# Attention scores of two heads at once on the two halves of TensorE's rows

## The reference

```
q, k, v = split(x @ qkv_w.T + qkv_b)          # per head 512 x 16
scores = q @ k.T * 16**-0.5, causal
attn = softmax(scores)
seq_out = attn @ v
x = layernorm(x + (seq_out + gated * mem_val) @ out_w.T + out_b)
x = layernorm(x + experts(x))
```

## Time and profile before

| | us |
|---|---|
| median of 3 runs | 828.99 (825.13 to 829.65) |
| profiled execution | 834.11 |
| its span | 832.4 |
| TensorE busy | 734.4 (88%) |
| VectorE busy | 603.8 (73%) |
| ScalarE busy | 351.0 (42%) |
| GpSimd busy | 422.3 (51%) |
| mean granted TensorE clock | 0.946 |

### The profile page before, as it was taken

The page is one execution under the profiler, slowest core; times in us unless marked ns, Lnnn a source line. Parts: engine busy times, 40 slices in busy tenths (PEclk is TensorE's granted clock), DMA queues, the critical chain, the costliest instruction groups (busy, mean ns, idle before and its releaser), DMA issues.

```text
span 832.4 us, 12395 instructions
## 1 busy us (share of the span) xinstructions
PE 734.4 (88%) x4004; PEld 495.0 (59%) x4004; DVE 603.8 (73%) x2105; ACT 351.0 (42%) x701; POOL 422.3 (51%) x334
## 2 busy tenths in 40 slices
PE   6993998898898998999898998878899899998995
PEld 3452655565565666565565664446677676776774
DVE  2344776778878888889688877736777877787785
ACT  2211555446454545555455555842242242232410
POOL 9200894996665676668476893424134042240410
PEclk9995999999998999999899997899999999999998
DMA  7899589675564574655734747220220302303000
GB/s 274 257 234 165 127 142 144 163 115 104 130 102 84 133 119 100 152 85 138 139 69 105 139 87 170 73 101 2 77 85 18 101 10 93 102 1 102 26 24 27
DMA packets 60420, 89.88 MB, mean 108 GB/s; under 512 B 8234, under 2 KB 37316, under 8 KB 60356
## 3 DMA queue, kind: packets, MB, share of 16 engines
q1 hardware_dynamic: 60356, 89.09, 47.7%
HBM read 54.72 MB, written 33.82 MB: 106 GB/s over the span
## 4 chain that ended last, share of the span: by engine, by line
PE 47%; DVE 23%; DMA 10%; POOL 9%; ACT 4%; issue 4%; SPq 2%; ACTq 0%; POOLq 0%; DVEq 0%
PE ps L1256 15%; PE ps L374 8%; PE ps L338 7%; PE ps L327 6%; PE ps L315 6%; DVE ps L468 5%; DMA Wm<-mem_scratch 3%; DVE Ob L516 3%; DMA Q<-MT 3%; DVE A L1390 3%; ACT X L1242 2%; PE ps L1221 2%; PE ps L232 1%; POOL Pr L612 1%; DVE Z L1276 1%
## 5 line engine op out<-in xcount | busy, mean ns | idle before, releaser
L468 DVE CUSTOM_DVE_ANT_0 ps<-ps,mask 128x256 f32<-128x256 f32 (+3 forms) x512 | 236.9, 509 | 31.8 <-PE ps L315 31.0
L411 ACT ACTIVATE Pr<-ps 128x512 f32<-128x512 f32 (+2 forms) x384 | 190.1, 528 | 114.8 <-PE ps L327 110.6
L327 PE MATMUL ps<-Q,K 98*128 98x256 f32 (+2 forms) x512 | 173.2, 380 | 28.9 <-DMA Q<-MT 21.9
L315 PE MATMUL ps<-K,Q 96*128 96x256 f32 (+2 forms) x512 | 157.9, 355 | 23.2 <-DVE nmax L468 22.5
L1256 PE MATMUL ps<-ew_hi,XT 128*128 128x512 f32 x512 | 176.2, 403 | 0.0
L1390 DVE SCALAR_TENSOR_TENSOR A<-ps,cw,A 128x256 f32<-128x256 f32 x256 | 123.6, 483 | 48.5 <-PE ps L1256 36.0
L327 PEld LDWEIGHTS ps<-Q,K 98*128 98x128 f32 x512 | 94.1, 197 | 104.8 <-ACT Pr L411 61.0
L612 POOL TENSOR_SCALAR_AFFINE_SELECT Pr<-Pr 128x512 f32<-128x512 f32 x128 | 88.3, 704 | 103.2 <-ACT Pr L411 100.8
L315 PEld LDWEIGHTS ps<-K,Q 96*128 96x128 f32 x512 | 103.0, 203 | 45.8 <-DVE nmax L468 28.3
L1256 PEld LDWEIGHTS ps<-ew_hi,XT 128*128 128x128 f32 x512 | 97.0, 189 | 21.2 <-issue 0.3
L1256 PE MATMUL ps<-ew_rest,XT 128*128 128x512 f32 x256 | 101.2, 395 | 0.0
(11 more groups left out here) (190 smaller groups left out, 1049.2 us busy)
## 6 DMA issues: line engine op xcount, KB each, us to landing
qk_scratch<-HL SPq DMA_DIRECT2D x32, 512.0 KB, 3.2
Q<-qk_scratch SPq DMA_DIRECT2D x96, 128.0 KB, 4.4
K<-qk_scratch SPq DMA_DIRECT2D x96, 128.0 KB, 5.7
Pr<-xT SPq DMA_DIRECT2D x8, 512.0 KB, 7.0
xraw<-xT SPq DMA_DIRECT2D x8, 512.0 KB, 6.4
mem_scratch<-Rl SPq DMA_DIRECT2D x16, 256.0 KB, 7.5
mv_scratch<-MV SPq DMA_DIRECT2D x32, 128.0 KB, 1.8
Wm<-mem_scratch SPq DMA_DIRECT2D x16, 256.0 KB, 9.3
```

Source lines behind the costliest of these rows:

```text
L315: last = nc.tensor.matmul(o, Q[0:STACK, hh, P * i:P * i + P], K[0:STACK, hh, 0:n], start=True, stop=True)
L327: last = nc.tensor.matmul(o, K[0:STACK + 2, hh, P * kt:P * kt + P], Q[0:STACK + 2, hh, T - n:T], start=True, stop=True)
L411: nc.scalar.activation(probs(g % 2, kt, heads[0], len(heads)), src, ACT.Exp, scale=SCALE).then_inc(s_exp, 1)
L468: last = nc.vector.tensor_tensor_reduce(out=scores, in0=scores, in1=mask[:, T - w:T], scale=1.0, scalar=NEG, op0=ALU.add, op1=ALU.max, acc ...
```

## The change

Scores use 64-row halves of the array. `STACK` is 48: head pairs stand one in rows 0 to 49 and one in rows 64 to 113 of `Q` and `K`, which have half as many column blocks. TensorE goes through the units in pairs (u, u + 1), and the two units' matmuls alternate between the halves and write to different banks. Max scores have four banks instead of three, so the outputs are turned in the values' bank and the maxima in the projections' bank. A pair of exp scores waits for all exponentials before it.

A projection is two pieces of three matmuls, at units 0 and 2, and 6 and 8, instead of one of six at units 4 and 10. Turning the maxima (unit 4) and turning the outputs (unit 8 instead of 10) stay on TensorE's list; the first now waits for VectorE's part of the projection before it. `HL`, `xhi` and `xlo` are held twice; the x split of a batch is done half a batch earlier. On VectorE the projection's part comes at units 4 and 10 instead of 5 and 11, the turned maxima at 5 instead of 4, and the normalising at 9 instead of 10. SyncE stores the two halves of `HL` apart, builds `Q` and `K` with eight DMAs a group instead of six (the same bytes), and writes the rows of maxima with four instead of two. The opening's memsets of `Q` and `K` shrink to two small ones of `K`.

```diff
-STACK = 96
+STACK = 48
+HALF = 64
-        S_ps, ST_ps = ps[0:2] + ps[7:8], ps[2:4]
-        O_ps, OT_ps, J_ps = ps[4:7]
-        M_ps = OT_ps
+        S_ps, ST_ps = [ps[0], ps[1], ps[7], ps[5]], ps[2:4]
+        O_ps, J_ps = ps[4], ps[6]
+        OT_ps, M_ps = O_ps, J_ps
...
-            return (2, [2 * (u - 8), 2 * (u - 8) + 1]) if u < 10 else (3, [2 * (u - 10), 2 * (u - 10) + 1])
+            return (2, [u - 8, u - 6]) if u < 10 else (3, [u - 10, u - 8])
+
+        def stacked(t, hh, n):
+
+            return t[HALF * (hh % 2):HALF * (hh % 2) + n, hh // 2, :]
...
         def pe_exp_scores(pe, b, g, u):
-            kt, heads = unit_parts(u)
-            n = max(T - P * kt, 2 * P)
+
             if u == 0:
-                need(pe, s_mrow[g], 32, b, 32)
-            need(pe, s_exp, PU, b, UNITS * g + u - 1)
-            for c, h in enumerate(heads):
-                hh = GROUP * g + h
-                o = ST_ps[u % 2][:, c * 256:c * 256 + n]
-                last = nc.tensor.matmul(o, K[0:STACK + 2, hh, P * kt:P * kt + P], Q[0:STACK + 2, hh, T - n:T],
-                                        start=True, stop=True)
-            last.then_inc(s_st, 1)
+                need(pe, s_mrow[g], 64, b, 64)
+            need(pe, s_exp, PU, b, UNITS * g + u)
+            for c in range(len(unit_parts(u)[1])):
+                for v in (u, u + 1):
+                    kt, heads = unit_parts(v)
+                    hh = GROUP * g + heads[c]
+                    n = max(T - P * kt, 2 * P)
+                    ins = nc.tensor.matmul(ST_ps[v % 2][:, c * 256:c * 256 + n],
+                                           stacked(K, hh, STACK + 2)[:, P * kt:P * kt + P],
+                                           stacked(Q, hh, STACK + 2)[:, T - n:T], start=True, stop=True)
+                    if c == len(heads) - 1:
+                        ins.then_inc(s_st, 1)
...
-        def pe_turn_max(pe, b, g):
+        def pe_turn_max(pe, b, g, projected):
             need(pe, s_max, PU, b, UNITS * (g + 1))
             need(pe, s_mt, 2 * NG, b, 2 * g)
-            need(pe, s_on, NG, b, g - 2)
+            pe.wait_ge(s_lo, projected)
...
+        def pe_project(pe, b, j, k, turned=0):
+
+            if j == 0 and k == 0:
                 need(pe, s_xlo, 1, b, 1)
-            need(pe, s_lo, 8, b, j)
...
+            if k == 0:
+                need(pe, s_lo, 8, b, j)
+                need(pe, s_mt, 2, turned, 0)
...
-                for u in range(UNITS):
+                for u in range(0, UNITS, 2):
                     pe_exp_scores(pe, b, g, u)
                     on, ng, nu = ahead(g, u)
                     if not (last and on):
                         pe_max_scores(pe, b + on, ng, nu)
-                    if u in (0, 2, 4, 6) and not (first and g == 0):
+                    if u < 8 and not (first and g == 0):
                         pe_values(pe, pb, pg, u // 2)
-                    if u in (4, 10) and not last:
-                        pe_project(pe, b + 1, 2 * g + u // 10)
+                    if u == 8 and not (first and g == 0):
+                        pe_turn_out(pe, pb, pg)
+                    if u in (0, 2, 6, 8) and not last:
+                        pe_project(pe, b + 1, 2 * g + u // 6, (u // 2) % 3, NG * b + g + 1 + u // 6)
                     if u == UNITS - LEAD and not (last and g == NG - 1):
-                        pe_turn_max(pe, b + (g + 1) // NG, (g + 1) % NG)
-                    if u == 10 and not (first and g == 0):
-                        pe_turn_out(pe, pb, pg)
+                        pe_turn_max(pe, b + (g + 1) // NG, (g + 1) % NG, min(8 * (b + 1) + 2 * g + 1, 8 * NB))
...
-                need(act, s_scr[(j - 1) % 4 // 2], 32, b, (0, 16, 32, 16)[j])
+                need(act, s_scr[j % 2], 64, b, 32 * (j // 2))
...
-                    if g == 0 and u == 0 and not last:
-                        dve_split_x(dve, b + 1)
-                    if u in (5, 11) and not last:
-                        dve_project(dve, b + 1, 2 * g + u // 11)
-                    if u == UNITS - LEAD and not (last and g == NG - 1):
+                    if u in (4, 10) and not last:
+                        dve_project(dve, b + 1, 2 * g + u // 10)
+                    if u == UNITS - LEAD + 1 and not (last and g == NG - 1):
                         dve_turned_max(dve, b + (g + 1) // NG, (g + 1) % NG)
-                    if u == 10 and not (first and g == 0):
+                    if u == 9 and not (first and g == 0):
                         dve_normalise(dve, pb, pg)
+                    if (g, u) == (1, 11) and b < NB - 2:
+                        dve_split_x(dve, b + 2)
...
             for r in range(2):
-                sp.dma_start(Q[STACK + r:STACK + r + 1, GROUP * g:GROUP * g + GROUP, :].rearrange(
-                    "o h (i t) -> o (h i) t", i=QT).bitcast(F32), MT[:, g % 2, r, :].bitcast(F32)).then_inc(s_mrow[g], 16)
+                for a in range(2):
+                    row = HALF * a + STACK + r
+                    sp.dma_start(Q[row:row + 1, 2 * g:2 * g + 2, :].rearrange("o c (i t) -> o (c i) t", i=QT).bitcast(F32),
+                                 MT[2 * QT * a:2 * QT * a + 2 * QT, g % 2, r, :].bitcast(F32)).then_inc(s_mrow[g], 16)
```

More of the change, by code:

```diff
@@ L19 @@
 GROUP = 4
-STACK = 96
+STACK = 48
+HALF = 64
+BROWS = 96
 VW = 17
@@ L305, in pe_max_scores @@
         def pe_max_scores(pe, b, g, u):
[L306 to L308 removed]
             if u == 0:
[L310 removed]
+                need(pe, s_stack[g], 128, b, 128)
             need(pe, s_max, PU, b, UNITS * g + u - 2)
[L312 to L315 removed]
@@ L316, in pe_max_scores @@
-            last.then_inc(s_s, 1)
+            for c in range(len(unit_parts(u)[1])):
+                for v in (u, u + 1):
+                    rank, heads = unit_parts(v)
+                    i, hh = QT - 1 - rank, GROUP * g + heads[c]
+                    n = max(P * (i + 1), 2 * P)
+                    ins = nc.tensor.matmul(S_ps[v % 4][:, c * 256:c * 256 + n], stacked(Q, hh, STACK)[:, P * i:P * i + P],
+                                           stacked(K, hh, STACK)[:, 0:n], start=True, stop=True)
+                    if c == len(heads) - 1:
+                        ins.then_inc(s_s, 1)
@@ L621, in sp_projected @@
             if j < 4:
-                need(sp, s_lo, 8, b, j + 1, apart=True)
-                sp.dma_start(qk_scratch[b, j], HL[:].bitcast(F32)).then_inc(s_scr[j // 2], 16)
+                for s, done in ((0, s_hi), (1, s_lo)):
+                    need(sp, done, 8, b, j + 1, apart=True)
+                    sp.dma_start(qk_scratch[b, j, :, s], HL[j % 2][:, s].bitcast(F32)).then_inc(
+                        s_scr[j % 2], 16)
             else:
@@ L951, in project, with scores @@
                 dve_project(dve, 0, j)
-            def scores(u0):
+            def scores(u0, u1):
                 if u0 == 0:
-                    dve.wait_ge(s_cst, 2)
-                for u in range(u0, u0 + 3):
+                    dve.wait_ge(s_cst, 1)
+                for u in range(u0, u1):
                     dve_max(dve, 0, 0, u)
@@ L1003, in project, with scores @@
                 if j == 4:
-                    pe.wait_ge(s_cst, 2)
-                pe_project(pe, 0, j)
-            def scores(u0):
+                    pe.wait_ge(s_cst, 1)
+                for k in range(KT):
+                    pe_project(pe, 0, j, k)
+            def scores(u0, u1):
                 if u0 == 0:
@@ L1011, in scores @@
                     pe.wait_ge(s_wr, 4)
-                for u in range(u0, u0 + 3):
+                for u in range(u0, u1, 2):
                     pe_max_scores(pe, 0, 0, u)
@@ L1018, in _ @@
             pe.wait_ge(s_p1g, 2)
-            pe_turn_max(pe, 0, 0)
-            for u in range(LEAD):
+            pe_turn_max(pe, 0, 0, 8)
+            for u in range(0, LEAD, 2):
                 pe_max_scores(pe, 0, 1, u)
```

133 lines of the change are left out of this document (73 added, 60 removed).

## The result

The changed kernel takes 862.85 us (median; 859.10 to 867.23), the kernel before 829.32 us beside it (825.13 to 831.29). The ratio is 1.041, with an interval from 1.034 to 1.049. (Some executions of a kernel fall in a slower state; medians and ranges in this document are of all executions, ratios and their intervals of the fast ones alone.) The prediction was 819.0 with a range up to 858, so both its sign and its range were wrong. The profiled execution took 867.2 us, its span is 865.4; 33.0 us more than the span before.

The account below looks back on a forecast made before the run. PE's work was taken to bound quiet groups, with 7.3 us a batch of other waits. From 834.1 us profiled, -4 (seven batches), -2 (opening) and -4 (last batch) gave 824.1, so median 819; own range 805 to 832, with rivals 785 to 858.

Parts of the forecast that it names:

- Full overlap of the halves: Score matmuls on the two 64-row halves run two at a time: 2.6 us a group instead of 5.3.
- Rival 4: The halves don't run at once in the scores: 1.6 us a group, +45, 865 us; chance 0.08.
- 0.15 for a pair of 256 columns: In PE's scores, two 256-column matmuls with both weight loads cost 0.15 us, between 0.12 and 0.24.
- Steps and groups at the full clock: Six steps per attention group: 13.7 us with HL, 12.9 with MV, 14.6 for a batch's first; 54.1 a batch.
- rival 1: Shorter rounds in the attention groups: about 12.4 us a group and fewer waits, 34 us, 785; chance 0.25.
- closed round: Each score pair waits for both exponentials before it: 1.75 us a round, giving back what PE saves.
- Clock, "0.6" us a batch: The sum's term for a colder clock in the attention batches: 0.6 us a batch.
- Rival 2: PE's idle time cools the attention stage's clock to 0.85: 0.9 us a group, 25 us, 845; chance 0.17.
- Rows of maxima, "0.4 us a batch": Four row DMAs instead of two bring the maxima late to the scores: 0.4 us a batch.
- Other waits, 3.7 us a batch gone: Of 7.3 us a batch, the earlier x split saves 2.5 and two HL buffers 1.2; 3.6 remain.
- Opening, -2: Two HL buffers shorten ACT's waits for HL's store in the opening: -2 us, bounds 0 and -3.5.
- Last batch, -4: Without projections in the last batch's steps, groups take 12.3 us against 13.8: -4 taken of 6.

Follow-up runs that it names:

- e6: e5 with each score matmul over all 128 rows (opened order, no overlap, computes something else): 836.32 us, ratio 1.010 to the kernel before.
- e1: The changed kernel with each score matmul over all 128 rows, same order, waits and DMAs, no overlap (computes something else): 847.88 us, ratio 1.026.
- e5: e4 with both scores of a step from heads on the same 64 rows, one after the other: 965.14 us, ratio 1.168.
- e8: e6 with the second group's eight transfers into Q and K moved behind the four rows of maxima: 828.60 us, ratio 1.001.
- e2: The changed kernel with zero-weight matmuls over 128 rows in PE's idle time at steps 4 and 10: 852.90 us, ratio 1.032.
- e3: e2 with the zero-weight matmuls over 64 rows instead of 128: 858.03 us, ratio 1.039.
- e4: The changed kernel with units one by one, exp scores overlapping max scores of the other half, turning and second projection's pieces moved: 893.04 us, ratio 1.079.

## Why the prediction was wrong, step by step

- **Full overlap of the halves: right.** Two exp scores of 512 columns span 0.49 us together (506.71), as long as one alone in the earlier trace rows (0.50), and two of 384 columns on the two halves start 4 ns apart (386.677 and 386.681). Rival 4 is out.
- **0.15 for a pair of 256 columns: slightly too much, and the page's objection didn't come.** Four max scores of 256 columns and the change to the values' form fit between 507.02 and 507.38, 0.36 us, where the forecast's terms give 0.38. Four exp scores of 256 columns start in pairs at 515.761, 515.981 and the scores behind them at 516.101, so a pair in a stream costs 0.12. Their four weight loads span 0.30 us together:

```profile
515.76 0.30 PEld L346 LDWEIGHTS ps<-Q,K 50*128 50x128 f32 x4 [0.38 <-issue]
```

  The Trainium skill's rule for weight loads ("TensorE: Matmul & The Clock Gate", section "LDWEIGHTS (loading the stationary operand)") gives 107 ns for one load of 128 columns, 0.43 us for four in series (an estimate). The measurement decides: the loads of a pair, into different halves, are recorded 3 ns apart and run at once. The prediction's objection had put two loads in series.
- **Steps and groups at the full clock: right.** Step 0 measured 2.55 us for 2.63; PE idle at step 4 behind DVE, 0.77 us; a quiet group with MV 12.67 us for 12.9. PE's work in the quiet group is 10.96 us, forecast 10.6. So rival 1 is out too: it wanted 12.4 as the mean, and the shortest group of these 28 takes 12.66. The closed round was seen correctly as what eats the halved scores; e6 against e1 puts it at 11.6 us of the whole.
- **Clock, "0.6" us a batch: the step that failed.** Rival 2 named the right mechanism and stated the bound from which the change ends slower, but it read the clock off the last batch of before (0.85) and blamed idle time alone. The sum took 0.6 us a batch, a sixth of the rival's own 4 x 0.9 = 3.6. Measured, the stage has 0.83 and the start of the last batch 0.75. The missing fact is that with scores on half the rows the clock holds less well than with scores on all of them, with or without overlap (e5 against e6, 0.69 against 0.96): in the changed kernel 15 of the 17 falls between 85 and 500 us stand behind pauses of 0.9 to 1.4 us, several of them the wait for DVE's HL at step 4 that rival 2 had pointed at, while e1 passes its pauses of 0.94 us in front of a group at the full clock. The time at the low clock went from 10% to 34%, and step 0 takes 4.57 us there for 2.55. Rival 2's price was of the right size: against e1 the mean group is 0.57 us longer and the quiet one 0.88 shorter, so 1.45 us a group for 28% more at the low clock, where it had 0.9 for 20%. What failed is the chance and the term of the sum. Against the same order on full rows (e1), the halves cost 15.0 us net, although they save PE 1.4 us in each group.
- **Rows of maxima, "0.4 us a batch": too small.** Mean groups by their place in the batch, in us:

| | first | second | third | fourth |
|---|---|---|---|---|
| forecast, the steps alone | 14.6 | 13.7 | 12.9 | 12.9 |
| before | 16.2 | 15.2 | 14.1 | 13.7 |
| changed | 15.7 | 16.7 | 16.7 | 13.4 |
| e1, full rows, closed rounds | 15.4 | 16.4 | 14.7 | 13.8 |
| e6, full rows, opened | 14.0 | 16.7 | 14.7 | 13.3 |
| e8, e6 with the rows earlier | 14.4 | 14.3 | 15.5 | 13.5 |

  At a full clock (e1, e6) it is the second group that is long, and e8's move takes 2.4 us out of it and puts 0.8 on the third. With four DMAs and eight in front of them the waits were 18.7 us in e1, and the move in e8 gave back 7.7 us, 1.1 a batch. In the changed kernel itself PE's waits for these rows are 18.0 us over all groups, 8.6 of them in the opening, so most of their lateness must be hidden behind other delays, which is argued and not shown.
- **Other waits, 3.7 us a batch gone: not seen.** e6 has all of it (HL and the split inputs twice, two pieces) with an open order and a clock of 0.96, and is 7 us *slower* than the kernel before. Whatever two HL buffers and the earlier split saved, something in the same edit used up. The rows' waits (26.4 us for 9.4) are the part that shows, and with them cut down (e8, 828.60) the kernel is level with the one before. No run takes the buffers, the pieces and the DMAs apart.
- **Opening, -2: wrong sign, +3.7.** In the opening's timeline of the changed kernel ACT still waits twice for a store of HL, which is now two transfers on the one queue and frees its buffer with the second:

```profile
22.12 0.69 ACT L438 ACTIVATE HL<-ps,qkb 128x512 fp32r<-128x512 f32 x1 [2.81 <-DMA qk_scratch<-HL]
27.13 0.69 ACT L438 ACTIVATE HL<-ps,qkb 128x512 fp32r<-128x512 f32 x1 [2.85 <-DMA qk_scratch<-HL]
...
31.70 3.39 SPq L668 DMA_DIRECT2D Q<-qk_scratch  x4
...
42.42 1.22 PE L331 MATMUL ps<-K,Q 48*128 48x512 f32 x4 [3.73 <-DMA K<-qk_scratch]
43.57 6.32 PE L238 MATMUL ps<-Pr 128*128 128x512 f32 x8
...
51.70 3.70 PE L238 MATMUL ps<-Pr 128*128 128x512 f32 x8
```

  The first transfers into Q start at 31.70 (28.83 before), PE waits 3.73 us for the last of K, and the eight memory matmuls behind it then take 6.32 us instead of 3.70: the granted clock from 40 to 60 us is 0.83, where it was 1.00 before. This is one execution; e2 and e3, with the same opening, reach their first scores at 80.37 and 81.89 us, so the opening costs 2 to 4 us more.
- **Last batch, -4: wrong sign, +3.6.** The forecast reckoned its rounds at the full clock; its first three groups (519.38 to 564.40) are granted 0.66. But the clock is not what lengthens them: e1 is granted 0.89 there and takes 44.75 us for the same three groups, against 45.02. e6, with the opened order, takes 42.77 at 0.92, and the kernel before 41.40. So most of it goes with the closed round and what e6 shares with the changed kernel.

The sum of the runs, in medians of kernels that were not all run side by side (before was 827.8 to 829.3 beside each): before 829; the buffers, pieces and DMAs on full rows in an open order +7 (e6); the closed round +12 (e1); half rows +15 (the changed kernel), which is what they cost with their saved work already taken off. The forecast had the second, and had the first and the third with the wrong sign or size.

What stays open: whether it is the number of rows or the changes of form that come with it; and why the opened, crossed order (e4) is granted even less than the closed one. Its pauses are of the same size (0.7 to 1.3 us), but its cold stretches last 10 to 17 us, those of the changed kernel 3 to 17. Its exp scores of 512 columns overlap with max scores of 256, so more of PE's time has only one half filled (12.0 us of work in a quiet group against 10.96); that fits, but was only argued. How the clock's loss splits between half rows and idle time in the changed kernel can't be said either, as each is needed: e1 removes one, e2 and e3 most of the other, and each brings the clock back almost alone.

## What to carry to other kernels

Before packing small contractions into parts of TensorE's rows, ask what clock the stage will be granted without its full-row matmuls: work saved on PE at 2.4 GHz may be paid for by all of PE's other work at 1.2 GHz. Price each way of ordering with the clock that the *new* mix will get, and take a cheap run (full rows, same order) to see it. Look at the pauses of PE too: here, ones that a kernel with full-row scores passed at the full clock cost the half-row kernel its clock. When one queue carries stores that free a buffer and rows that release the next group, each added or moved transfer is to be priced by who waits behind it, and a second buffer is what makes a move affordable.

## What the runs showed of the hardware

- With scores on 48 or 50 rows, PE busy 93% of 415 us, the granted clock was 0.69 (e5); on 128 rows in the same order, busy 89%, it was 0.96 (e6).
- In e5 the clock fell behind pauses of PE of 0.55 to 1.14 us and stayed low for 10 to 17 us; in e6 it fell behind pauses of 1.9 to 5.5 us and stayed low for 3 to 7.
- Zero-weight matmuls in idle time held the clock as well on 64 rows (0.94) as on 128 (0.95), in a kernel whose scores overlap on the halves (e3, e2; 0.83 without the filling).
- Four max scores of 256 columns on alternating halves, with the change of form behind them, took 0.36 us; a pair of exp scores of 256 columns in a stream 0.12 us, their weight loads starting 3 ns apart.
- Four row transfers of 4 KB each took 2.7 us to issue on SP, and 3.5 us right behind other transfers (e1); two of 8 KB took 1.23 in the kernel before.
